# Two self-attentions of a transformer kernel, worked batch behind batch instead of both together

## The reference, cut to what matters

```python
r = layernorm(x)                    # the residual of the block
h = ln(r, ln1_w, ln1_b)
q, k, v = (split_heads(h @ w + b) for w, b in ((q_w, q_b), (k_w, k_b), (v_w, v_b)))
a = softmax(causal(q @ k.T / sqrt(8))) @ v
r = r + merge(a) @ o_w + o_b
h2 = ln(r, ln2_w, ln2_b)
logits = h2 @ router_w              # 16 experts, two per token, then the experts
x = x + r + experts(h2, logits)
```

## Time and profile before

| what | us |
|---|---|
| median of 3 runs (lowest, highest) | 1254.61 (1251.87, 1260.2) |
| the profiled execution, its own time | 1259.82 |
| its span, first to last instruction | 1257.6 |
| PE busy, share of the span | 958.8 (76%) |
| DVE busy | 589.2 (47%) |
| ACT busy | 437.1 (35%) |
| POOL busy | 218.4 (17%) |
| granted TensorE clock, mean | 0.863 |

### The profile page before, as it was taken

One profiled execution on the slowest core, in us unless ns is written; L12 is line 12 of the kernel. 1 busy time (PEld: TensorE's weight loads), 2 busy tenths in 40 slices (PEclk: granted clock), 3 DMA queues, 4 the chain that ended last, 5 costly groups with the idle time before them and its releaser, 6 DMA issues. The chain is left out here.

```text
span 1257.6 us, 15487 instructions
## 1 busy us (share of the span) xinstructions
PE 958.8 (76%) x5556; PEld 645.7 (51%) x5561; DVE 589.2 (47%) x1312; ACT 437.1 (35%) x761; POOL 218.4 (17%) x243
## 2 busy tenths in 40 slices
PE   5872599833664638999778925999699988869998
PEld 3661244423653526677647811232266676756776
DVE  4867445351225462311766667576244446632111
ACT  2331155501331203343343310577432233424443
POOL 0334010005033200000372340001000011431100
PEclk9996589965996868999888965799889988989999
DMA  8001511001730000110000006020001111110111
GB/s 343 1 1 48 128 40 40 7 29 39 209 110 9 1 0 1 38 46 17 26 1 1 2 9 167 20 58 2 1 13 38 38 35 51 51 34 18 34 33 34
DMA packets 33264, 55.71 MB, mean 44 GB/s; under 512 B 3697, under 2 KB 25398, under 8 KB 32817
## 3 DMA queue, kind: packets, MB, share of 16 engines
q1 hardware_dynamic: 32176, 52.88, 13.8%
q0 software_dynamic: 1024, 1.98, 0.6%
HBM read 44.81 MB, written 9.96 MB: 44 GB/s over the span
## 5 line engine op out<-in xcount | busy, mean ns | idle before, releaser
L2089 PE MATMUL psum<-xT_all,wexp 128*128 128x512 f32 x400 | 185.1, 608 | 1.3 <-issue 0.7
L1380 DVE TENSOR_REDUCE arena<-psum 128x2 f32<-128x1024 f32 (+3 forms) x128 | 127.6, 1022 | 85.8 <-PE psum L1917 49.9
L949 ACT ACTIVATE arena<-psum 128x512 f32<-128x512 f32 (+3 forms) x256 | 115.8, 515 | 74.9 <-PE psum L1930 37.6
L697 POOL TENSOR_TENSOR rstd<-var,held 128x8 f32<-128x8 f32 (+2 forms) x24 | 51.9, 2180 | 415.8 <-DVE var L1148 392.1
L2089 PEld LDWEIGHTS psum<-xT_all,wexp 128*128 128x128 f32 x400 | 74.6, 196 | 79.1 <-issue 73.2
L1914 PE MATMUL psum<-arena 72*128 72x512 bf16 (+3 forms) x256 | 85.1, 406 | 25.2 <-DMA arena<-parts_q 19.1
L2104 PEld LDWEIGHTS psum<-wexp,arena 128*128 128x128 f32 x800 | 94.2, 192 | 16.2 <-issue 14.4
L1849 PE MATMUL psum<-values_out_all,arena 128*128 128x128 f32 x560 | 78.5, 289 | 26.5 <-ACT arena L921 26.2
L727 POOL TENSOR_TENSOR arena<-arena,small 128x616 f32<-128x616 f32 x56 | 67.9, 1216 | 173.2 <-DVE small L1327 173.1
L2104 PE MATMUL psum<-wexp,arena 128*128 128x128 f32 x800 | 94.7, 275 | 0.9 <-DVE r_res L1619 0.9
L1927 PE MATMUL psum<-arena 75*128 75x512 bf16 (+3 forms) x256 | 77.1, 368 | 13.4 <-DMA arena<-arena 11.5
(11 more groups left out here) (264 smaller groups left out, 1483.9 us busy)
## 6 DMA issues: line engine op xcount, KB each, us to landing
wexp<-experts SPq DMA_DIRECT2D x32, 514.0 KB, 3.5
parts_k<-arena SPq DMA_DIRECT2D x12, 384.0 KB, 3.7
arena<-parts_k SPq DMA_DIRECT2D x48, 96.0 KB
arena<-parts_q SPq DMA_DIRECT2D x48, 96.0 KB
arena<-experts SPq DMA_DIRECT2D x8, 514.0 KB, 3.8
wexp<-experts SPq DMA_DIRECT2D x9, 384.0 KB, 3.1
held<-packed SPq DMA_DIRECT2D x1, 2375.0 KB, 15.4
held<-packed SPq DMA_DIRECT2D x1, 2264.5 KB, 20.8
```

What stands on the lines that cost most here:

```text
L697: pool.tensor_tensor(dst, src, half[0:src.shape[0], 0:n], ALU.pow).then_inc(done, 1)
L949: act.activation(p_self[:, n % 2, kt % 2, j, lo:S], bank(t_bank("keys", c, k), lo, S), ACT.Exp, scale=DS ** -0.5).then_inc(ut_ok, 1)
L1380: dve.tensor_reduce(top[:, x % 2, qt, j:j + 2], src, AX_X, ALU.max, negate=True).then_inc(us_ok, 1)
L2089: mm(bank(c, 0, BANK), wexp[:, side, c * P:(c + 1) * P], xT_all[:, b * S:(b + 1) * S], start=True, stop=True).then_inc(h_ps, 1)
```

## The change

Everything around the two self-attentions is cut by batch.

- Batch 0's tiles are done when the cross-attention's loop is at half 8 of 16. Its norms, turn, projections and splits are put into the rest of that loop, at fixed iterations n on each engine (`LAST_OF_BATCH` is 7, `ADD` is 5). POOL does the two powers there, over four columns each.
- Batch 1's norms follow the loop. Its turn, projections and splits are put into the ticks -9 to -4, between the scores of batch 0.
- k is still split by DVE. q is now split by POOL: `split_queries`, two subtractions and two casts of 128x512. ACT writes the rest next to the first part from PSUM, so the first subtraction reads SBUF.
- The projection of the context, the adds, the norm, the turn and the router are cut by batch as well and get ticks 19, 22, 24 and 27 behind the last tick in which a batch's last group starts: batch 0's lie in ticks 43 to 51, batch 1's behind the last keys. `MOMENTS` goes to 83.
- Placement: parts and rests move to wexp and values_out_all (so SP issues the two first expert loads only once the parts are stored, in front of the first `load_top`), the exponents of layer 0 move behind the rings, POOL's memsets are of the key ring's 4096 float32 columns with a value whose two halves are both one in bf16 (before the padding) and twice 2048 columns of wide values (in iteration 3, and once all halves are turned), and layers 0 and 2 use bank 6 alone for their sums, with a wait for the add of the tile before.

```diff
@@ POOL, xattn
+                u = l // 2 if l in (0, 2) else None
+                if u is not None:
+                    pool.wait_ge(x_xTp, 2 * l + 2)
+                    if l == 2:
+                        pool.wait_ge(qrstd_ok, NT)
+                    pool.memset(U["k"][64:96, :], ONES_IN_PAIRS).then_inc(ones_set, 1)
+                    pool.wait_ge(ones_set, u + 1)
+                    pool.wait_ge(vw_ps, FIRST_W[l] + 4)
                 pool.memset(E4[l][:, :, HALF:CHUNKED], 0.0).then_inc(pads_ok, 1)
                 for n in range(HALVES[l]):
                     at = FIRST_HALF[l] + n
+                    if u is not None and n == 3:
+                        pool.memset(U["v0"], 1.0).then_inc(wide_set, 1)
+                    if u is not None and n == LAST_OF_BATCH + ADD - 1:
+                        batch_tokens(0, a_stat, SELF_AT[l] + 1, a_rstd)
+                    if u is not None and n == LAST_OF_BATCH + ADD:
+                        batch_tokens(0, b_stat, B * u + 1, b_rstd)
                     pool.wait_ge(e_inv, at + 1)
...
@@ POOL, selfattn
-                all_tokens(a_stat, 2 * u + 1, a_rstd)
-                all_tokens(b_stat, u + 1, b_rstd)
-                pool.wait_ge(b_rstd, u + 1)
-                pool.memset(k_ring[64:96, :, :, :], 1.0).then_inc(ones_set, 1)
-                pool.wait_ge(ones_set, u + 1)
-                pool.memset(U["v"], 1.0).then_inc(wide_set, 1)
+                l = 2 * u
+                split_queries(u, 0)
+                batch_tokens(1, a_stat, SELF_AT[l] + 2, a_rstd)
+                batch_tokens(1, b_stat, B * u + 2, b_rstd)
+                pool.wait_ge(pT_ps, FIRST_HALF[l] + HALVES[l])
+                pool.memset(U["v1"], 1.0).then_inc(wide_set, 1)
+                split_queries(u, 1)
...
+            def split_queries(u, b):
+
+                at = B * u + b + 1
+                pool.wait_ge(hi_ok, 2 * at)
+                step.then(pool.tensor_tensor(q_rest, q_rest, q_parts[:, 0, :], ALU.subtract))
+                pool.tensor_copy(q_parts[:, 1, :], q_rest).then_inc(q_split, 1)
+                pool.wait_ge(q_split, 2 * at - 1)
+                step.then(pool.tensor_tensor(q_rest, q_rest, q_parts[:, 1, :], ALU.subtract))
+                pool.tensor_copy(q_parts[:, 2, :], q_rest).then_inc(q_split, 1)
...
@@ SP, selfattn
                 store_split(u, 1)
                 split_stored(sp, u, 1)
+                for side in range(2):
+                    if u == 0:
+                        load0(side, side)
+                    else:
+                        load(2, side, side)
                 for x in range(GROUPS):
                     load_top(u, x)
...
@@ ACT, xattn
+                    if l in (0, 2):
+                        if n == LAST_OF_BATCH + 8:
+                            self_tokens(l // 2, 0, 7)
+                        if n == LAST_OF_BATCH + 9:
+                            self_projected(l // 2, 0, 0, 7)
+                        if n == LAST_OF_BATCH + 10:
+                            self_projected(l // 2, 0, 1, 0)
                     m = n - TURN
...
+            def self_projected(u, b, which, n):
+
+                parts, rest, own = ((k_parts, k_rest, "s0_k_b"), (q_parts, q_rest, "s0_q_b"))[which]
+                act.wait_ge(pj_ps, 3 * (B * u + b) + which + 1)
+                if b:
+                    split_stored(act, u, b - 1)
+                func, kw = (ACT.Identity, dict(bias=w(own))) if u == 0 else (ACT.Copy, {})
+                act.activation(parts[:, 0, :], bank(n, 0, BANK), func, **kw)
+                act.activation(rest, bank(n, 0, BANK), func, **kw).then_inc(hi_ok, 1)
...
@@ DVE, xattn (n is the iteration)
+                    if u is not None and n == LAST_OF_BATCH + ADD:
+                        self_moments(u, 0)
                     if n < HALVES[l]:
                         dve.wait_ge(sc_ps, at + 1)
...
+                    if u is not None:
+                        if n == LAST_OF_BATCH + ADD:
+                            self_residual(u, 0)
+                        if n == LAST_OF_BATCH + ADD + 1:
+                            self_normal(u, 0)
+                        if n == LAST_OF_BATCH + 10:
+                            split_keys(u, 0)
+                        if n == LAST_OF_BATCH + 11:
+                            self_values(u, 0, 1)
...
@@ DVE, ticks
+                    if tick == 6 - LEAD:
+                        split_keys(u, 1)
+                    if tick == 7 - LEAD:
+                        self_values(u, 1, 4)
...
+                    b = projected_at(tick)
+                    if b is not None:
+                        projected(b)
+                    b = scaled_at(tick)
+                    if b is not None:
+                        tokens_scaled(b)
+                    b = routed_at(tick)
+                    if b is not None:
+                        routed(b)
...
@@ PE, xattn
                     if half == 0:
-                        pe.wait_ge(x_done, (2 if l == 3 else 1) + NT * l + t)
+                        pe.wait_ge(x_done, (1 if l == 1 else 2) + NT * l + t)
...
+                    if l in (0, 2):
+                        if n == LAST_OF_BATCH + 8:
+                            self_turned(l // 2, 0, 7)
+                        if n == LAST_OF_BATCH + 9:
+                            self_projected(l // 2, 0, 0, 7)
+                            pe.wait_ge(e_sub, FIRST_HALF[l] + HALVES[l] - 1)
+                            self_projected(l // 2, 0, 1, 0)
+                            self_projected(l // 2, 0, 2, 1)
                     if n >= VALUE:
                         values(n - VALUE, at - VALUE)
...
@@ PE, ticks
+                    if tick == 3 - LEAD:
+                        self_turned(u, 1, 4)
+                    if tick == 4 - LEAD:
+                        self_projected(u, 1, 0, 5)
+                        self_projected(u, 1, 1, 6)
+                    if tick == 5 - LEAD:
+                        self_projected(u, 1, 2, 4)
+                    if tick == 8 - LEAD:
+                        pe.wait_ge(hi_ok, 2 * B * (u + 1))
+                        pe.wait_ge(v_in_ok, B * (u + 1))
                     a = pair_at(tick)
...
+                    b = projected_at(tick)
+                    if b is not None:
+                        project_batch(b)
+                    b = tokens_turned_at(tick)
+                    if b is not None:
+                        turn_tokens(b)
+                    b = routed_at(tick)
+                    if b is not None:
+                        router(b)
```

More of the change, by code:

```diff
@@ L439, in batch_turned_at, with batch_at, projected_at, scaled_at @@
             return x // 4 if x is not None and x % 4 == 3 else None
+        def batch_at(tick, after):
+            x = group_at(tick, after)
+            return x // 4 if x is not None and x % 4 == 3 else None
+        def projected_at(tick):
+            return batch_at(tick, 19)
+        def scaled_at(tick):
+            return batch_at(tick, 22)
+        def tokens_turned_at(tick):
+            return batch_at(tick, 24)
+        def routed_at(tick):
+            return batch_at(tick, 27)
         def keys_valued_at(tick):
             return tick // 2 - 2 if tick % 2 and 4 <= tick < TICKS + 4 else None
-        MOMENTS = range(-LEAD, TICKS + 10)
+        MOMENTS = range(-LEAD, TICKS + 20)
         s_place, t_place = {}, {}
@@ L457, in program @@
                 t_place["batch", batch_turned_at(tick_)] = len(t_place)
+            if projected_at(tick_) is not None:
+                s_place["project", projected_at(tick_)] = len(s_place)
+            if tokens_turned_at(tick_) is not None:
+                t_place["tokens", tokens_turned_at(tick_)] = len(t_place)
+            if routed_at(tick_) is not None:
+                s_place["router", routed_at(tick_)] = len(s_place)
         def s_count(u, *what):
@@ new lines, in xattn, with batch, self_moments, self_residual @@
+                dve.wait_ge(x_done, 2 + NT * (l + 1))
+            def batch(b):
+                return range(b * TB, (b + 1) * TB)
+            def self_moments(u, b):
+                held_in(dve, [1, 3][u])
+                dve.wait_ge(x_done, 2 + NT * 2 * u + TB * (b + 1))
+                moments(x_res, a_stat, tiles=batch(b))
+            def self_residual(u, b):
+                if u == 0 and b == 0:
+                    dve.wait_ge(zeros_out, 16 * (SLOTS // 1024))
+                dve.wait_ge(a_rstd, SELF_AT[2 * u] + b + 1)
+                scaled(r_res, x_res, tiles=batch(b))
+                moments(r_res, b_stat, rms=(u == 1), eps=[EPS_LN, 1e-6][u], tiles=batch(b))
@@ new lines, in self_normal, with split_keys @@
+            def self_normal(u, b):
+                dve.wait_ge(b_rstd, B * u + b + 1)
+                scaled(xn_self, r_res, rms=(u == 1), done=b_xn, tiles=batch(b), to=b * TB)
+            def split_keys(u, b):
+                at = B * u + b + 1
+                dve.wait_ge(hi_ok, 2 * at - 1)
```

(27 more changed lines are left out.)

303 lines of the change are left out of this document (149 added, 154 removed).

## The result

The changed kernel takes **1217.87 us** (median of 4 runs, 1216.37 to 1221.08), the kernel before 1255.46 on the same chip (1251.87 to 1260.2): ratio 0.9702, 95% interval [0.9663, 0.974]. On another chip it took 1218.74 (1217.56 to 1220.39), ratio 0.9697 [0.9674, 0.972]. The profiled execution took 1217.17, its span is 1215.1 (before 1257.6), its mean granted clock 0.877 (before 0.863). So the spans differ by 42.5 and the medians by 37.6, where the forecast had 53.6. (The profiled execution of the kernel before lay 4.4 above that kernel's median, so the medians are the fairer measure.) The prediction of 1201 was 17 too low; its range (1185 to 1223) holds the result.

The account below looks back on a forecast made before the run. No engine is full overall; gaps of 40.5 and 40.6 us, then leads and tails, cost time around both self-attentions. 25.0 + 25.4 + 6.0 + 5.2 - 4 - 4 = 53.6 off 1259.82 gives 1206, less 5.2: 1201; range 1185 to 1223.

Parts of the forecast that it names:

- the batches come apart: Both self-attentions: batch 0's first scores no longer wait for batch 1's chain; forecast 1201 us, chance 0.56.
- rivals 4 and 5: Rival 4: batches do not come apart, 1232, chance 0.06; rival 5: TensorE stays at 1.2 GHz through ticks, 1274, 0.03.
- rival 1: POOL's query splits, ahead of batch 1's rsqrts, take 7 to 10 each instead of 4.4; 1213 to 1225, chance 0.15.
- One sum bank instead of two. Cost 0: Cross-attention loop: PE waits for the previous tile's add, which is over at 62.80, before values at 63.10; cost 0.
- a few tenths per tile were the add later: Cross-attention loop: cost of the single sum bank per tile should the previous tile's add come later.
- The loops end over 8 later: Cross-attention loops: sign that the prediction is wrong, if they end over 8 us later.
- rival 3: Self-attentions: POOL's splits lock DVE out, up to 4.4 us more each; 1210, chance 0.07.
- The other way in is no later: Lead to first keys: pairs 0 to 7 end near 118, top parts split on POOL by 120.5, top row 121.8.
- cost 4: Ticks of each self-attention: batch 0's tail inside them costs 4 us, PE being the bound.
- The bounds 0 and 8: Ticks: lower and upper bounds in us on the cost of batch 0's tail, each self-attention.
- Project half of 2.02: Batch 1's tail: projection takes half of 2.02, part of a tail of 12.5 instead of 18.5 us.
- Rival 2: Lead and early ticks: TensorE's clock comes back sooner, 6 us each time; 1189, chance 0.13.

Follow-up runs that it names:

- the scaling ahead alone: Changed kernel with batch 0's scaled residual and normalised tokens on DVE ahead of their iteration's sum and reciprocal: 1216.29 us, ratio 0.9677.
- the run with the top rows ahead: Changed kernel with batch 1's key split behind pair 7, values first, and SP loading group 0's top rows before batch 1's stores and expert loads: 1214.76 us.
- the changed kernel once more: The changed kernel itself, unaltered, run and traced again for comparison on the experiments' chip: 1218.74 us.
- the run with both tails together: Changed kernel with batch 0's tail moved from ticks 43 to 51 to the tick ahead of batch 1's: 1217.71 us, ratio 0.9685.
- the four edits together: Changed kernel with spread norms and sooner tile 4 add, later key split, top rows loaded ahead, wide values' memset ahead of rsqrts: 1204.06 us, ratio 0.9579.

## Why the prediction was right, and where it was wrong

**Right: the batches come apart.** The first scores of batch 0 wait for its own loads (110.78) and not for batch 1's chain, the gap is gone, and the ticks are back at full clock from 155 and 760 on, so rivals 4 and 5 are out. First scores on 72 rows come at 110.78 and at 719.53 + 20.8 = 740.3 on the old time line (said: about 107 and 739; the loop ended 5.1 later than said in the first). The gain is 79% of the forecast's by the spans and 70% by the medians. No run takes the cutting by batch apart from POOL's splits of the queries and from the new placement; that the cutting is what closed the gap is read from the two traces. POOL's split takes 1.16 + 0.61 + 1.16 + 0.61 = 3.5 alone, 3.7 with gaps, where 4.4 was said, so rival 1 is out as well; its cast at 0.61 is cheaper than the 1.1 taken from the multiply. The rsqrt of four columns takes 1.01 as said.

**That the range held is luck in part.** Its upper end, 1223, was set by rival 1, which is out; what did go wrong (the loop and the lead) had no term of that size in it. And the misses offset each other: the loops and the steps to the first keys took 15.3 more than forecast, the ticks 6.3 less, the tails gave 2.0 less.

**"One sum bank instead of two. Cost 0" failed.** The row it rested on the earlier trace rows was from the middle of the loop, where nothing else is on DVE. At tile 4 the add stands behind batch 0's norms, and PE waited 4.42. The prediction had said "a few tenths per tile were the add later", and had put the norms on DVE itself: the two sentences were not held together. "The loops end over 8 later" stood among the prediction's own signs of being wrong, and they ended 12.5 and 9.5 later. The wait has a second price, the clock, 0.50 from 84 to 87. Removing the add's wait alone gave back 1.5, the scaling ahead alone 1.5, and both with the norms one half later 3.2. Of the 12.5 that the first loop's end moved, 9.2 remain then, against 7.4 forecast. PE waits 1.50 and 1.48 in that run for the tokens and their copy (84.89, 88.65), which the forecast had as running on.

**"I do not take that, but it is rival 3" failed.** The lock-out is real and reaches further than memsets. What it costs DVE in the first self-attention of the changed kernel: 0.87 and 0.86 beside the multiply, 1.26 beside the last memset, and 1.41 on batch 1's key split (3.65 instead of 2.24), 4.4 in sum. That this is rival 3's figure is chance: rival 3 had taken the length of POOL's split. And it isn't the splits of batch 0, and it isn't all on the path: removing the first two brought the first loop's end 1.5 sooner, removing the third brought the keys nothing. Once DVE's key split is moved, the lock-out falls on POOL's top rows, on the path (the run with the top rows ahead). The Trainium skill, SBUF — State Buffer, Who interferes with whom, says more than the sentence quoted before the run: DVE's copy, cast and tensor_scalar can enter the two-port modes, which contend with GpSimd, a DVE instruction with two SBUF inputs contends with one of GpSimd that reads SBUF, and whichever starts first keeps the ports to its end. The traces agree in each: tensor_scalar 1.11 to 1.97, cast 0.43 to 0.72, tensor_tensor on two SBUF operands 0.69 to 1.52, subtraction with a PSUM operand hardly, 0.80 each against 0.70 to 0.75; and POOL's cast behind DVE's start 0.61 to 1.01.

**"The other way in is no later" failed.** By the forecast pairs 0 to 7 would end 3.3 behind the last part's copy (114.7 to 118). They ended 7.7 behind it (120.6 to 128.3): maxima of 1.21 each, the split of 3.65 and the value copy in one queue. With the projections at the lower clock (0.9) that is 5.3 too late; from the maxima to the first keys it was then 6.8 where the forecast had 8.8, which gives 2.0 back. So the step from last add to first keys was 3.2 longer than forecast (3.6 in the second). Taking DVE's part away showed SP's queue to be as late, and the two together gave 1.8 and 2.2.

**Both ticks' "cost 4" was too high.** They grew by 0.7 and 1.0, in the trace of the changed kernel once more by 0.6 and 2.1. The bounds 0 and 8 had been written, and the middle was taken; by the run with both tails together batch 0's tail costs nothing there in the first and about 2.6 in the second.

**"Project half of 2.02" held at full clock only.** The eight matmuls of the tail took 2.05 in the trace shown, as long as sixteen in the earlier trace rows, at a clock of 0.55 for the tail (0.68 before). But the same eight took 1.54 and 1.13 in the trace of the changed kernel once more, and 1.13 twice with the four edits together. So about 1.0 of the 1.2 missing in the first tail is the clock of one execution. In that trace the tails are 5.3 and 5.0 shorter than before, where 6.0 and 5.2 were said.

**Rival 2 had a real price, but its condition did not come true.** The clock does not stay up by itself: 0.64 in the lead, 0.66 in the 20 us behind it. It was said to be worth 6 us each time; made to come back by added work it shortened the ticks by 5.0 and 4.8.

## What to carry to other kernels

When work is put into a loop "because the engine has room", look up who waits for that engine's next result before putting a price of zero on a buffer that was taken away; putting the waited-for add sooner was worth 4.6 us here, and with the pieces reordered and spread over the iterations it was 8. Where a start has several queues leading to it, one of them made faster shows nothing: move the second as well before giving the idea up. And look at the granted clock where TensorE comes out of a thin stretch into a full one: here it read 0.66 over the first 19.9 us of the full one and 0.52 over the first 12.3 us of the second. Added matmuls in the thin one shortened what follows by 5 us each time; the whole kept about 4 by the medians, and the intervals leave even that open.

## What was not expected of the hardware

- POOL's cast of 128x512 from float32 to bf16 takes 0.61, about half of its two-operand operations of that size (1.16).
- The lock-out between DVE and POOL goes both ways and can last until POOL's instructions end: two casts of DVE, 0.76 together, took 5.54, from 109.45 to the second memset's end. The other way round, POOL's small casts of 0.21 took 0.60 and 0.66 beside DVE's split.
- Behind a single wait of PE of 4.42 us in a full loop the granted clock read 0.50 (84 to 87), and 0.50 too with a wait of 2.83 in its place. In one of two traces of the same program it also read 0.66 from 45 to 50, in the other 1.00, with the same wait of 1.89 at 45 in both.
